# Feed-forward layers of the first sequence placed beside the second sequence's attention, and the first sequence's causal maximum mask on TensorE

## What is computed

```python
q = q * cos + _rotate_half(q) * sin; k = k * cos + _rotate_half(k) * sin
att = jnp.where(causal, einsum('bhtd,bhsd->bhts', q, k) * scale, finfo.min)
y = einsum('bhts,bhsd->bhtd', softmax(att), v)        # then @ w_proj
x = _layernorm(x + attn(x)); x = _layernorm(x + xattn(x, ctx, ctx, mask))
h = silu(_tlin(x, w1)) * _tlin(x, w2)                  # _tlin(x, w, s) = x @ w.T * s
h = gelu(_tlin(h, h1)); h = gelu(_tlin(h, h2))         # 1024 -> 1024, twice
x = _layernorm(x + _tlin(h, w3))
```

## Time and profile before

| | us |
|---|---|
| median of 3 runs | 971.66 (967.42 to 973.08) |
| the profiled execution | 979.19 |
| its span | 977.8 |
| TensorE busy (matmuls) | 882.5, 90% |
| VectorE, ScalarE, GpSimd busy | 538.2, 364.8, 363.0 |

### The profile page before, as it was taken

The page is one execution under the profiler, slowest core; times in us unless marked ns, Lnnn a source line. Parts: engine busy times, 40 slices in busy tenths (PEclk is TensorE's granted clock), DMA queues, the critical chain, the costliest instruction groups (busy, mean ns, idle before and its releaser), DMA issues. The chain is left out here.

```text
span 977.8 us, 13145 instructions
## 1 busy us (share of the span) xinstructions
PE 882.5 (90%) x4466; PEld 563.2 (58%) x4466; DVE 538.2 (55%) x1404; ACT 364.8 (37%) x770; POOL 363.0 (37%) x576
## 2 busy tenths in 40 slices
PE   5879999888889999999968789999998889999997
PEld 2545444334644788888745444543357257888886
DVE  3596788767676711441145967886167774116113
ACT  0314666454354421231103236665734443113110
POOL 4312224345345533353333122231362645335333
PEclk9965999769986999999979668997999699999999
DMA  9909201000000000000020000010000000000000
GB/s 305 336 7 401 72 2 46 2 1 1 2 5 0 1 1 1 1 1 1 22 94 1 1 2 2 2 45 2 1 1 4 3 1 1 1 0 22 1 1 24
DMA packets 15973, 34.61 MB, mean 35 GB/s; under 512 B 3483, under 2 KB 12392, under 8 KB 15720
## 3 DMA queue, kind: packets, MB, share of 16 engines
q1 hardware_dynamic: 15896, 33.63, 9.9%
HBM read 31.00 MB, written 13.63 MB: 46 GB/s over the span
## 5 line engine op out<-in xcount | busy, mean ns | idle before, releaser
L749 PE MATMUL bank<-hid_lo,ffn_w 128*128 128x512 f32 x512 | 202.2, 395 | 0.0
L878 ACT ACTIVATE prob<-bank 128x512 f32<-128x512 f32 (+3 forms) x384 | 164.2, 496 | 101.6 <-PE bank L550 100.9
L749 PE MATMUL bank<-hid_hi,ffn_w 128*128 128x512 f32 x512 | 201.6, 394 | 0.0
L1326 POOL TENSOR_TENSOR hid_lo<-act_raw,hid_hi 128x512 fp32r<-128x512 f32 x96 | 123.9, 1290 | 182.4 <-DVE hid_hi L1164 182.4
L1164 DVE CAST hid_hi<-act_raw 128x512 fp32r<-128x512 f32 x96 | 41.7, 435 | 212.4 <-ACT act_raw L964 211.3
L521 PE MATMUL bank<-k_t,q_t 64*128 64x512 f32 (+3 forms) x384 | 145.0, 496 | 13.0 <-DVE max_raw L1030 8.5
L1280 POOL TENSOR_SCALAR_AFFINE_SELECT prob<-prob 128x128 f32<-128x128 f32 x256 | 84.0, 344 | 180.5 <-ACT prob L878 177.9
L1030 DVE CUSTOM_DVE_ANT_0 bank<-bank,causal_bf 128x128 f32<-128x128 f32 (+3 forms) x256 | 122.3, 512 | 28.9 <-PE bank L521 26.8
L550 PE MATMUL bank<-q_t,k_t 64*128 64x512 f32 (+3 forms) x384 | 123.8, 438 | 0.9 <-issue 0.5
L964 ACT ACTIVATE act_raw<-bank,scales 128x512 f32<-128x512 f32 x64 | 44.2, 690 | 193.1 <-PE bank L749 193.1
L550 PEld LDWEIGHTS bank<-q_t,k_t 64*128 64x128 f32 x384 | 63.3, 211 | 82.5 <-ACT prob L878 47.5
(11 more groups left out here) (127 smaller groups left out, 1234.5 us busy)
## 6 DMA issues: line engine op xcount, KB each, us to landing
ffn_w<-scratch_h SPq DMA_DIRECT2D x2, 4096.0 KB, 23.2
ffn_w<-scratch_w SPq DMA_DIRECT2D x3, 1024.0 KB, 7.0
x_t<-in_x_t SPq DMA_DIRECT2D x2, 1024.0 KB, 5.2
x_tok<-in_x SPq DMA_DIRECT2D x2, 1024.0 KB, 5.5
out<-tok SPq DMA_DIRECT2D x16, 128.0 KB, 1.8
q_t<-max_rows SPq DMA_DIRECT2D x64, 4.0 KB
qx_t<-max_rows SPq DMA_DIRECT2D x64, 4.0 KB
w_qkv<-in_w_qkv SPq DMA_DIRECT2D x1, 768.0 KB, 6.9
```

Of the source, the lines that this page charges most:

```text
L749: o = mm(out[:], w_view(2 + layer, dt)[:, k, P * m:P * (m + 1)], view(src[part][:, k]), start=k + part == 0, stop=(k, part) == (KH - 1, 1))
L878: act.activation(prob[4 * (s % 2) + j][:, 0:n], S_BANK[j][:, 0:n], ACT.Exp, scale=SCALE).then_inc(S["exp_done"], 1)
L1326: pt(dst[1][:, r % 8], act_raw[n % 3][:], dst[0][:, r % 8].bitcast(F32), ALU.subtract).then_inc(S["act_lo"], 1)
```

## The change

The loop is gone; both sequences are written out, with arrays (and most semaphores' counts) of their own (`q` is the sequence, 0 or 1). The first runs projections, attention and cross-attention as before, all norm tiles included. Then its feed-forward layers are cut into single products and dealt out by a table (`PLAN`: chunk, layers, first and last slot, slot of a row of Gelu passes, first slot of the split into parts) over slots: Q for projections, S for attention steps, X for cross-attention steps, E behind them. In a slot TensorE does its four scores and maxima, then the slot's products (`f_products`), then the values. The second sequence's own feed-forward layers follow as before.

Further parts. The feed-forward products take banks 4 and 5, so in the second sequence scores 0 and 2 share bank 2, scores 1 and 3 bank 3. Silu is written as a tanh (scaled halves) with two passes on VectorE. h2's results are copied and get their Gelu in one row of eight passes, with a table load ahead and one behind where Exp follows. The weights come through a ring of six tiles of 512 KB for the first sequence, each twice (once a chunk), and into home places for the second; they are checked in a region that the second sequence uses later. Transfers of tokens and context for the second sequence start during the first. And in the first sequence 128 of the 192 maxima get the mask from TensorE: two more bf16 products of 128 columns into the same bank (`ident_half` times `causal_half`), and a plain reduction.

```diff
-        with nc.Fori(0, BATCH) as b:
-            with nc.Block() as block:
-                build_sequence(nc, block, b, shared, S)
-            nc.all_engine_barrier(sems_to_clear=range(first, last + 1))
-        nc.sync.wait_ge(out_done, 16 * NT * BATCH)
...
+S_BANKS = ((2, 3, 4, 5), (2, 3, 2, 3))
...
+SHARED = (6, 4)
+F_BANKS = (4, 5)
...
+SLOTS = [("Q", t) for t in range(NT + V_LAG)] + [("S", s) for s in range(FIRST_STEP, S_END)] + \
+        [("X", s) for s in range(-XSTAGE, FFN_STEP)] + [("E", i) for i in range(4)]
+SLOT_AT = {slot: n for n, slot in enumerate(SLOTS)}
+END_SLOT = len(SLOTS) + 4
...
+GROUPS = [(c, layer, m) for c in range(NC)
+          for layer, m in [(w, m) for m in range(KH) for w in ("w1", "w2")] + [("h1", m) for m in range(KH)]
+          + [("h2", m) for m in range(KH)] + [("w3", i) for i in range(4)]]
...
+PLAN = [
+    (0, ("w1", "w2"), ("Q", 2), ("Q", 12), None, None),
+    (0, ("h1",), ("S", -18), ("S", -5), None, ("S", -4)),
+    (0, ("h2",), ("S", 0), ("S", 27), ("S", 29), ("S", 29)),
+    (0, ("w3",), ("S", 33), ("S", 37), None, None),
+    (1, ("w1", "w2"), ("S", 38), ("S", 47), None, None),
+    (1, ("h1",), ("S", 49), ("X", -7), None, ("X", -6)),
+    (1, ("h2",), ("X", -2), ("X", 7), ("X", 8), ("X", 9)),
+    (1, ("w3",), ("E", 0), ("E", 3), None, None),
+]
...
+    for _j, (n, i) in enumerate(_work):
+        _k = max(_a + _j * (_b - _a + 1) // len(_work), F_DONE.get(n - len(F_BANKS), -1) + 1)
+        F_MM[_k].append((n, i))
+        F_DONE[n] = _k
...
+    if _burst:
+        IN_BURST.add((_c, _layers[0]))
+        F_BURST[SLOT_AT[_burst]].append((_c, _layers[0]))
+    if _split:
+        for _m in range(KH):
+            F_SPLIT[SLOT_AT[_split] + _m // 2].append((_c, _layers[0], _m))
+for _n, (_c, _layer, _m) in enumerate(GROUPS):
+    if _layer == "w2":
+        F_SPLIT[F_DONE[_n] + 1].append((_c, "gate", _m))
...
+RING = 6
...
+RING_FILL = [[r for r in range(RING, NC * PIECES) if F_DONE[RING_LAST[r - RING]] + 1 == k] for k in range(END_SLOT)]
...
+            diagonal = q == 0 and k1 == P * (qt + 1)
+            m = mm(out[:, 0:k1 - k0], qkt(q, p, 0)[r, P * qt:P * (qt + 1)], qkt(q, p, 1)[r, k0:k1], start=True, stop=not diagonal)
+            if diagonal:
+                for i in range(2):
+                    m = mm(out[:, k1 - k0 - P:k1 - k0], L["ident_half"][r, i], L["causal_half"][r, i], start=False, stop=i == 1)
+            m.then_inc(S["max_mm"], 1)
...
+        def score_bank_free(q, name, s, j):
+            if S_BANKS[q][j] in S_BANKS[q][:j]:
+                wait(pe, q, name, 4 * s + j - 1)
+            elif s:
+                wait(pe, q, name, 4 * (s - 1) + max(i for i in range(4) if S_BANKS[q][i] == S_BANKS[q][j]) + 1)
...
+        def f_bank_free(n):
+            if n < len(F_BANKS):
+                return
+            c, layer, m = GROUPS[n - len(F_BANKS)]
+            if layer == "w1":
+                pe.wait_ge(S["f_gate1"], KH * c + m + 1)
+            elif layer == "w2":
+                pe.wait_ge(S["f_gate2"], KH * c + m + 1)
+            elif layer == "w3":
+                wait(pe, 0, "o_mul", 4 * c + m + 1)
+            else:
+                pe.wait_ge(S["f_evac"], 24 * c + 8 * LAYER_NUMBER[layer] + m + 1)
...
+            if i == 0:
+                f_bank_free(n)
+            if i == 0 or layer == "w3" and i == 8:
+                r = ring_uses(n)[i // 8]
+                pe.wait_ge(ring_in[r % RING], 16 * (r // RING + 1))
+            if layer in ("w1", "w2"):
+                tile = ring[ring_uses(n)[0] % RING]
+                o = mm(out[:], view(tile_w12(tile[:], m, int(layer == "w2"), k), True),
+                       view(x_hl[0][part][:, k, CHUNK * c:CHUNK * (c + 1)]), start=i == 0, stop=i == last)
...
+                else:
+                    tile = ring[ring_uses(n)[0] % RING]
+                    o = mm(out[:], view(tile_h(tile[:], k), True), view(hid_f[part][:, k]), start=i == 0, stop=i == last)
+            if i == last:
+                o.then_inc(S["f_mm"], 1)
+        def f_products(slot, exact):
+            if slot is None:
+                return
+            for n, i in F_MM[slot]:
+                f_product(n, i, exact)
...
+        def second_sequence(exact):
+            for k, (stage_name, s) in enumerate(SLOTS):
+                if stage_name == "Q":
+                    projections(1, s, k, exact)
+                if stage_name == "S":
+                    attention(1, s, k, exact)
+                if stage_name == "X":
+                    cross_attention(1, s, k, exact)
+                if stage_name == "E":
+                    f_products(k, exact)
+            ffn(exact)
...
+        def f_work(slot):
+            for n in F_AFTER[slot]:
+                c, layer, m = GROUPS[n]
+                if layer in ("w2", "w3"):
+                    continue
+                act.wait_ge(S["f_mm"], n + 1)
+                out = bank[F_BANKS[n % 2]]
+                if layer == "w1":
+                    act.activation(raw[m][:], out[:], ACT.Tanh, scale=half_scale[:, 0, m:m + 1]).then_inc(S["f_evac"], 1)
+                elif (c, layer) in IN_BURST:
+                    act.activation(raw[m][:], out[:], ACT.Copy).then_inc(S["f_evac"], 1)
+                else:
+                    act.activation(raw[m][:], out[:], ACT.Gelu, scale=scales[:, 1 + LAYER_NUMBER[layer], m:m + 1]).then_inc(S["f_evac"], 1)
+            for c, layer in F_BURST[slot]:
+                for m in range(KH):
+                    act.wait_ge(S["f_evac"], 24 * c + 8 * LAYER_NUMBER[layer] + m + 1)
+                    act.activation(raw[m][:], raw[m][:], ACT.Gelu, scale=scales[:, 1 + LAYER_NUMBER[layer], m:m + 1]).then_inc(S["f_gelu"], 1)
...
+        def f_split(c, layer, m):
+            n = 24 * c + 8 * LAYER_NUMBER[layer] + m
+            if layer == "gate":
...
+                if c and m == 0:
...
+                if m == 0:
+                    dve.wait_ge(S["f_mm"], PER_CHUNK * c + 16 + 8 * LAYER_NUMBER[layer])
...
+        def f_work(slot):
+            for n in F_AFTER[slot]:
+                c, layer, m = GROUPS[n]
+                out = bank[F_BANKS[n % 2]]
+                if layer == "w1":
+                    dve.wait_ge(S["f_evac"], 24 * c + m + 1)
+                    dve.scalar_tensor_tensor(out=raw[m][:], in0=raw[m][:], scalar=1.0, in1=out[:],
+                                             op0=ALU.add, op1=ALU.mult).then_inc(S["f_gate1"], 1)
+                if layer == "w2":
+                    dve.wait_ge(S["f_gate1"], KH * c + m + 1)
+                    dve.wait_ge(S["f_mm"], n + 1)
+                    dve.scalar_tensor_tensor(out=raw[m][:], in0=out[:], scalar=half_scale[:, 1, m:m + 1], in1=raw[m][:],
+                                             op0=ALU.mult, op1=ALU.mult).then_inc(S["f_gate2"], 1)
+                if layer == "w3":
+                    dve.wait_ge(S["f_mm"], n + 1)
+                    out_stats(0, 4 * c + m, out[:, 0:D])
+            for c, layer, m in F_SPLIT[slot]:
+                f_split(c, layer, m)
```

More of the change, by code:

```diff
@@ L830, in _ @@
+        for s in range(-XSTAGE, XNORM + NT + 4):
+            if s == -XMAX:
+                pe.wait_ge(S["flag_set"], 1)
+            cross_attention(0, s)
+        first_sequence_done(pe)
+        wait(pe, 1, "x_t_in", 16)
         with pe.register("low_bits_any") as found:
@@ L1116, in x_reduce @@
+        def x_reduce(q, p, u):
             n = 3 * p + u
```

1425 lines of the change are left out of this document (827 added, 598 removed).

## The result

The changed kernel takes 1003.04 us (median of four, 998.99 to 1004.41) where the kernel before takes 972.31 beside it: 1.032 times as long, with a 95% interval of 1.0273 to 1.0368. The prediction was 972 us, that is no change, within 935 to 1003. The change is slower, by 31 us, and the time lies at the very edge of the range, 0.04 us outside it. The profiled execution took 1004.38 us with a span of 1002.7, against 977.8 before. The other 6 us of the 31 come from the profile before, which was 0.7% above its kernel's median, while this one is 0.1% above.

The account below looks back on a forecast made before the run. TensorE was taken to bound the kernel, with 68 us of unevenly spread room while the second sequence attends. 977.8 - 180.2 + 6 + 172 + 2 = 977.6 us of span, 972 us as median; range 935 to 1003.

Parts of the forecast that it names:

- what the removed block saves: First sequence's feed-forward row of 180.20 us goes, 6 us of its cross-attention come back; 174 us saved.
- The sign named for the mask: First sequence's last token tile ready at about 332; 320 if reductions were the bound, 345 if the mask's products were.
- steps 0 to 28: Second sequence's attention, a full stretch: 29.9 us of products cost their length less some 5 us, +25.
- the cross steps with their tail: Second sequence's cross steps 0 to 7 +21 us, the tail +11, then w3's 64 products alone +8.
- the one for the projections: Second sequence's projections: 64 products of 14.9 us with 3 us of gate waits; 28.7 grows to 41 us, +12.
- the head: Second sequence's attention steps -20 to -1: 128 products, 29.9 us, VectorE the bound; 37.6 becomes 60 us, +22.
- The bank term: Two score banks in the second sequence: free beside maxima, later 14 us more over 15 steps, about half waiting before.
- The Gelu row: Step 29: eight Gelu passes and two table loads, 8.1 us, ahead of Exp on ScalarE; about 7.5 us reach TensorE.
- The mask's gain on VectorE: First sequence's diagonal maxima save 0.17 us each; 8 us gained in the first three pairs, mask in all +2.
- rival (b): Two score banks pace all 48 attention steps; steps 0 to 28 about 1.1 us longer each, 1002 us median; chance 0.20.
- Rival (a): Second sequence's overlap fills better, clock stays full, waits fall beside products: 933 us median; chance 0.30.
- (c): Weight tiles of the ring of six come late, 1 us for each of 38 refills: 1009 us median; chance 0.05.

Follow-up runs that it names:

- The reordering: Changed kernel with tanh ahead of the V evacuation and earlier staging of the first pair, in the second sequence's projections: 988.40 us, ratio 1.0115.
- the two mask runs: On one chip, the changed kernel unaltered, 1005.65 us, and the changed kernel with the mask on VectorE in both sequences, 998.02 us.
- the version with all edits: Changed kernel, mask on VectorE, tanh and staging earlier, four score banks in steps 34-41 and cross steps 1-5, last Gelu row dealt out: 968.41 us.
- the changed kernel's second run: The changed kernel itself, unaltered, run again beside other variants on one chip: 1005.65 us, ratio 1.0261 to the kernel before.

## Why the prediction was wrong

What bounds the kernel, and what the removed block saves, was right: -172.6 us measured for -172 (174 saved, 2 for the mask), but its two parts miss by about 4 us each and cancel, which is luck: the mask costs 5.7 us for 2, and the rest gives back 178 for 174. The sign named for the mask came out just as luckily (the second sequence starts at 331.73, and "about 332" was said). What was given back holds the 6.6 us of lower clock that the profile before has in its first sequence, which the forecast didn't see. Right too was the main reason why nothing is gained: the second sequence's steps 0 to 28 were full, and 29.9 us of products cost 28.6 there, where I had 25. Of the "some 5 us" that I took off for half clock or VectorE's arrears, the traces show the 3.4 of the clock, and at like clock the products cost 2 us more than their length. And the cross steps with their tail, 39.2 for 40.

**The step that failed most is the one for the projections**, +12 with "3 us of waits for the gate". It measured +25.3, so it makes up 13 of the 25 us by which the spans miss the forecast. I had counted what the gate costs the engines that compute it, "two VectorE passes behind one ScalarE pass", and not where the ScalarE pass stands in its queue: behind the evacuation of V, which waits for TensorE's own later products. From one gate to the next it was 4.7 to 5.6 us (371.00, 375.73, 381.36), TensorE had something else to do for 3 to 4 of them, and at the end the staging of the first pair waited behind the gates. The waits of these two kinds are 5.5 us each. The reordering gave 12 us of it back, and 2 more in the head.

**The bank term was too small in its second half.** "14 us more, of which about half was waiting before". The 14 us, 0.93 for each of 15 steps, are what the kernel before with two banks shows in steps at the higher clock, 0.93 each. But the half didn't go away: in the changed kernel, at a clock of 1.00, four banks took back 8.6 us in steps 34 to 41 alone, where I had counted about 7 for all fifteen. The Gelu row made TensorE wait 7.37 us for my 7.5; steps 29 to 32 grew by only 5.6 us for it, because the profile before has them at a clock of 0.70, in 17.3 us, and the version with two banks at 1.00 in 14.1. The whole stretch from step 29 on missed by 4.4 us.

**The mask's gain on VectorE.** "Mean saving 0.17 us" a unit was the difference of mean durations, of rows that overlap. From start to start it is 0.03. The 8 us gained in the head were never there; the price that I took on TensorE, 0.14 a unit, was rather too high (0.10, below). Bounds of -8 and +12 held the 5.7.

The other terms are 3 to 4 us too low each (head 26.0 for 22, steps 0 to 28, up to the cross scores 39.4 for 36). Why, no run took apart. All misses from the projections to the cross scores have one sign, and the prediction named the place: how the waits of two engines add in one step, "worth 20 us either way". They added upwards here.

**The rivals.** The time is that of rival (b), 1002 us, but by chance, for its mechanism isn't there: with two banks alone steps 0 to 28 are longer by about 1 us. Rival (a)'s sign, a clock near 1 throughout, came nearly true (0.88 to 0.97 up to the feed-forward block, where it was 0.62 to 1.00), and its time did not. The higher clock paid only where TensorE itself was late, 6.5 us in steps 3 to 5 and 29 to 31; most of the low clock before lay where TensorE waited for others, in the head (0.69) and in the cross steps (0.62), and there nothing got shorter. (c), late ring tiles, is nowhere in the trace as the end of a wait of TensorE. Of the signs named ahead: steps 0 to 28 at 4.26 us (said 4.2), the four scores of step 36 2.23 us (said over 2), the gap at the Gelu row 7.4 us (said 7), cross steps at 6.8 (said 6.6), the feed-forward block 173.6 (said 176), its first product at 829 (said 802). The chance of "slower", 0.36, looks too low in hindsight: most terms had more ways to be too low than too high.

What stays open: why the head, steps 0 to 28 and the stretch before the cross scores cost 3 to 4 us more than forecast; whether four banks at step 29, or products between its scores, would hide part of the Gelu row, which was not tried; and how much of the 7.6 us between the two mask runs, beyond the 5.7 of the first sequence, is the clock or noise.

## What to carry to other kernels

Work laid beside other work cost about its length where the engine was full, and more than that where its side steps (an activation, a gate, a copy) entered the queues of other engines behind something that waited for the first engine. So before pricing an overlap, follow one result of it through each queue and write down what stands ahead of it; a round trip found this way may be removed by a change of the order alone, as here, 14 us. Price instructions by the distance between starts, not by mean durations, where they follow each other closely. And count the resource that the overlap borrows (here two of four banks) at every place where it was in use, also where nothing is overlapped.

## What the runs showed of the hardware

VectorE's casts and its passes from SBUF to SBUF with a scalar (L1509, L1393) stand still while GpSimd runs an elementwise pass of 128x512 (lines of the version with all edits): L1393 takes 0.40 us alone, 1.14 beside it, ending 0.15 us behind GpSimd's, and always 0.40 once GpSimd's passes are gone; where such a pass starts as one of GpSimd's two ends, as at 777.05, it keeps its 0.40 and GpSimd's pair is longer (2.72 us for 2.49); VectorE's elementwise passes that read PSUM (L1405, L1458) keep their 0.41 throughout. The Trainium skill (SBUF — State Buffer, SBUF: two separate sides) has such a lock on a port pair that the two engines share, held for a whole instruction; the trace agrees, with these numbers. It matters here because the change puts GpSimd's passes beside VectorE's norm work.

The two mask products of a unit (bf16, 128 columns each) take 0.10 us of TensorE at the higher clock (from 127.15 to 127.25 in the changed kernel's second run, and 0.096 as the median of 77 such places); at the lower clock the four of two units together take 0.19. The pass behind a table load starts as the load ends (573.07 and 1.28 give 574.35, and it starts at 574.36), and the load as the pass ahead of it ends (573.05 and 573.07).

The read of the accumulator behind VectorE's fused mask and maximum overlaps both neighbours: 0.70 and 0.15 by duration, 0.61 to 0.64 from start to start.
